# Routing of a mixture-of-experts layer: logits with the gate as the stationary operand, 32x32 transposes on VectorE, and a new order of work

## What is computed

```python
scores = jax.nn.softmax(xf @ gate_w.T, axis=-1)
topk_w, topk_i = jax.lax.top_k(scores, 2)
topk_w = topk_w / (topk_w.sum(-1, keepdims=True) + 1e-20)
combine = jnp.zeros((T, 8)).at[jnp.arange(T)[:, None], topk_i].add(topk_w)
h1 = jax.nn.relu(jnp.einsum('th,ehf->tef', xf, w1) + b1)
eo = jnp.einsum('tef,efh->teh', h1, w2) + b2
y = jnp.einsum('te,teh->th', combine, eo)
shared = jax.nn.relu(xf @ sw1 + sb1) @ sw2 + sb2
return y + shared
```

## Time and profile before

| | before |
|---|---|
| median of 3 runs | 638.89 us (638.68 to 639.09) |
| profiled execution, device time | 639.33 us |
| profiled execution, span | 637.5 us |
| PE busy | 606.4 us, 95% of the span |
| DVE, ACT, POOL busy | 441.2, 402.4, 368.5 us |
| mean granted TensorE clock | 0.981 |

### The profile page before, as it was taken

The page is one execution under the profiler, slowest core; times in us unless marked ns, Lnnn a source line. Parts: engine busy times, 40 slices in busy tenths (PEclk is TensorE's granted clock), DMA queues, the critical chain, the costliest instruction groups (busy, mean ns, idle before and its releaser), DMA issues.

```text
span 637.5 us, 17017 instructions
## 1 busy us (share of the span) xinstructions
PE 606.4 (95%) x6275; PEld 529.2 (83%) x6275; DVE 441.2 (69%) x1322; ACT 402.4 (63%) x1346; POOL 368.5 (58%) x545
## 2 busy tenths in 40 slices
PE   8886889999999999999999999999999999999796
PEld 7775779898889888898889889888888889887674
DVE  5453666768777776868777776867777786867553
ACT  3466557676866667676866667675866667666400
POOL 2566437565674847565674847566683856546300
PEclk9988969999999999999999999999999999999999
DMA  6000030120303030120303021030313020020303
GB/s 231 1 27 4 22 97 25 38 97 2 110 26 108 26 105 29 32 103 1 110 26 108 25 100 35 25 111 1 109 27 108 26 81 28 15 97 2 109 2 119
DMA packets 15460, 37.43 MB, mean 59 GB/s; under 512 B 1809, under 2 KB 4241, under 8 KB 15377
## 3 DMA queue, kind: packets, MB, share of 16 engines
q1 hardware_dynamic: 15376, 36.34, 17.1%
HBM read 33.13 MB, written 3.20 MB: 57 GB/s over the span
## 4 chain that ended last, share of the span: by engine, by line
PE 75%; ACT 7%; DVE 7%; POOL 5%; issue 3%; DMA 1%; SPq 0%; ACTq 0%; POOLq 0%; DVEq 0%
PE ps_fill L414 13%; PE ps_fill L416 11%; PE ps_fill L415 11%; PE ps_mix L642 9%; PE ps_dots L630 9%; PE ps_av L650 7%; PE ps_fill L778 6%; PE ps_fill L570 4%; ACT ex L803 3%; DVE aT L1086 3%; POOL sum L1227 2%; PE ps_fill L770 2%; ACT sq L811 2%; POOL sum L1230 1%; PE ps_fill L761 1%
## 5 line engine op out<-in xcount | busy, mean ns | idle before, releaser
L803 ACT ACTIVATE ex<-ps_dots,negmax 128x92 f32<-128x92 f32 x384 | 123.7, 341 | 7.0 <-DVE negmax L1070 6.5
L1227 POOL TENSOR_TENSOR sum<-sq 92x384 f32<-92x384 f32 x64 | 64.2, 1003 | 80.3 <-ACT sq L811 79.5
L1221 POOL TENSOR_TENSOR probs<-ex,rinv 128x552 f32<-128x552 f32 x64 | 71.0, 1109 | 29.7 <-DVE rinv L1076 29.7
L642 PE MATMUL ps_mix<-mixk,probs 64*92 64x64 f32 x1536 | 79.2, 251 | 5.5 <-DVE aT L1086 5.4
L642 PEld LDWEIGHTS ps_mix<-mixk,probs 64*92 64x92 f32 x1536 | 70.7, 163 | 16.3 <-issue 10.7
L1167 DVE SCALAR_TENSOR_TENSOR act<-ps_fill,b_neg,spread 128x368 f32<-128x368 f32 x123 | 67.9, 591 | 19.9 <-PE ps_fill L416 15.1
L803 ACT ACTIVATION_READ_ACCUMULATOR ex<-ps_dots,negmax 128x1 f32 x384 | 81.4, 212 | 0.0
L630 PE MATMUL ps_dots<-xT,yT 128*64 128x92 f32 x1536 | 75.6, 249 | 5.5 <-ACT ex L803 4.9
L630 PEld LDWEIGHTS ps_dots<-xT,yT 128*64 128x64 f32 x1536 | 65.0, 139 | 11.6 <-ACT ex L803 8.8
L1086 DVE TENSOR_TENSOR aT<-ps_mix,arstd 92x384 f32<-92x384 f32 x128 | 64.9, 547 | 7.1 <-ACT arstd L821 5.2
L1244 POOL TENSOR_TENSOR xT<-xT_split_hi,xT_split_lo 128x368 f32<-128x368 f32 x16 | 15.6, 973 | 86.1 <-DVE xT_split_lo L1146 86.1
(11 more groups left out here) (190 smaller groups left out, 1566.9 us busy)
## 6 DMA issues: line engine op xcount, KB each, us to landing
spread<-weights SPq DMA_DIRECT2D x64, 368.0 KB, 5.6
xin<-in_x SPq DMA_DIRECT2D x16, 372.0 KB, 3.2
out<-fT SPq DMA_DIRECT2D x16, 184.0 KB, 1.9
act<-w_raw SPq DMA_DIRECT2D x1, 576.0 KB, 6.5
w_sb<-w_raw SPq DMA_DIRECT2D x1, 576.0 KB, 7.2
qkv<-qk_raw SPq DMA_DIRECT2D x1, 512.0 KB, 5.2
spread<-tok_raw SPq DMA_DIRECT2D x1, 256.0 KB, 3.4
spread<-wv_raw SPq DMA_DIRECT2D x1, 256.0 KB, 5.4
```

The lines of the kernel that those rows point to most:

```text
L642: last = pe.matmul(ps_mix[0:N, half, DH * c:DH * c + DH], probs[rows, (s - 1) % 2, c, :], mixk[rows, :, :].rearrange("p g i -> p (g i)"), ...
L803: last = act.activation(ex[:, s % 2, c, :], ps_dots[:, c // HALF, o:o + N], ACT.Exp, bias=negmax[:, c:c + 1], accum_out=sums[:, s % 2, c:c ...
L1221: pool.tensor_tensor(probs[:, s % 2, :, :], ex[:, s % 2, :, :], rinv[:, s % 2, :].unsqueeze(2).broadcast_to([128, CHUNKS, N]), ALU.mult).t ...
L1227: pool.tensor_tensor(sum4[:, :, :, :], sq[:, :, 0:4, :], sq[:, :, 4:8, :], ALU.add)\
```

## The change

The logits are two products with the gate (padded to 128 columns with zeros) as the stationary operand; x moves, 384 columns each time. They come out with experts in partitions: partitions 0 to 7 hold the gate's high half, 8 to 15 its low half. DVE turns 32x32 blocks (`transpose`), so that 32 partitions hold 12 blocks of rows, adds the two halves, and makes the choice on 12 x 8 = 96 elements per partition. R3 writes three copies of the weights side by side and turns them back with a second `transpose` into `flat`, from which SP stores as before. CT is now a copy on ACT (the high half); a new step CB on DVE makes `combT` out of `flat` and its high half in one instruction. The fill CT and its transposes are gone. `b2_all` has its three copies in partitions 0 to 23 and no longer at 0, 32 and 64; its split takes other instructions. `STEPS`, `BANKS`, `ORDER_0` and `ORDERS_END` are new lists.

```diff
-N_ROUTE = 18
-ROUTED = {"RT": 2, "R2": 12, "R3": N_ROUTE}
+N_ROUTE = 19
+ROUTED = {"RT": 3, "R2": 13, "R3": N_ROUTE}
+SIDE = 32
+BLOCKS = WP // SIDE
-ROWS_CT = (COPIES - 1) * COPY + E
+ROWS_CT = COPIES * E
+STEPS = [('dots', 0), ('mix', 0), ('max', 0), ('sq', 0), ('exa', 0), ('exb', 0), 'Z1', 'Z0', 'Z6', ('av', 0), ('inv', 0),
+ 'Z3', ('ev', 0), ('rstd', 0), 'Z8', 'XE', 'H0', ('scale', 0), 'Z4', 'Z2', ('dots', 1), ('av', 1), ('ev', 1),
+ ('mix', 1), ('sq', 1), ('max', 1), ('exa', 1), 'Z5', 'XO', 'OP', ('exb', 1), ('rstd', 1), 'shift', ('inv', 1), 'V3',
+ ('scale', 1), ('dots', 2), 'TH2', ('max', 2), 'TK', ('mix', 2), 'NH2', 'TH', 'Z7', ('exa', 2), ('exb', 2), 'TX2',
+ 'NH', ('av', 2), 'H1', ('dots', 3), ('sq', 2), 'RT', 'V2', ('inv', 2), 'R2', 'TX', 'R3', 'YF', ('rstd', 2),
+ ('scale', 2), ('ev', 2), 'Y2', 'Y0', 'Y4', 'XS', 'CT', ('max', 3), 'Y6', ('mix', 3), 'Y1', 'CB', ('sq', 3),
+ ('exa', 3), ('exb', 3), 'Y5', 'hold', 'Y3', 'Y7', ('rstd', 3), ('inv', 3), ('scale', 3), ('av', 3), 'BS', 'V0',
+ ('ev', 3)]
-BANKS = [['Z5', 'Z6', 'Z1', 'TK', 'TH', 'V3', 'TX', 'Y5', 'Y1', 'Y0'],
- ['Z3', 'Z8', 'Z7', 'TH2', 'TX2', 'RT', 'CT', 'Y3', 'Y4', 'V0'],
- ['Z2', 'Z0', 'OP', 'Z4', 'V2', 'YF', 'Y6', 'Y2', 'Y7', 'BS']]
+BANKS = [['Z1', 'Z3', 'Z2', 'V3', 'TH', 'TX', 'Y0', 'Y5', 'BS'],
+ ['Z6', 'Z8', 'OP', 'TH2', 'TX2', 'RT', 'YF', 'Y4', 'Y3', 'V0'],
+ ['Z0', 'Z4', 'Z5', 'TK', 'Z7', 'V2', 'Y2', 'Y6', 'Y1', 'Y7']]
...
- ['Z1', 'Z0', 'Z8', 'T2', 'Z3', 'T4', 'T5', 'T6', 'T7', 'YF']]
+ ['Z3', 'Z0', 'Z1', 'T7', 'T4', 'T2', 'T5', 'Z8', 'T6', 'YF']]
...
-        gate_both = sb("gate_both", [128, 2 * E], F32R)
+        gate_both = sb("gate_both", [128, 128], F32R)
...
-                if step == "CT":
-                    pe.wait_ge(route, N_ROUTE * (g + 1))
+                if step == "YF":
+                    pe.wait_ge(combine_ready, g + 1)
...
-                    for t in range(TILES):
-                        x_hi, x_lo = [m[:, R * t:R * t + R] for m in x2T]
-                        o = 2 * E * t
-                        pe.matmul(ps[:, o:o + 2 * E], x_hi, gate_both[:, :], start=True, stop=False)
-                        last = pe.matmul(ps[:, o:o + E], x_lo, gateT[0], start=False, stop=True)
-                    last.then_inc(done, 1)
-                elif step == "CT":
-                    transposes(step, G, [(ps[:, R * t:R * t + R], combine[:, t, :], ident) for t in range(TILES)])
+                    hi, lo = [m[:, :] for m in x2T]
+                    pe.matmul(ps[:, 0:WP], gate_both[:, :], hi, start=True, stop=False)
+                    pe.matmul(ps[:, 0:WP], gate_both[:, :], lo, start=False, stop=True).then_inc(done, 1)
...
+                if step == "CT":
+                    act.wait_ge(weights_flat, g + 1)
+                    at_least(act, combine_ready, g)
+                    act.activation(flat_high[:, :], flat[0:ROWS_CT, 0:W], ACT.Copy).then_inc(combine_high, 1)
-                elif step == "CT":
-                    wait_filled(act, step, G)
-                    act.activation(flat[:, :], ps[0:E, 0:W], ACT.Copy).then_inc(weights_flat, 1)
-                    act.activation(combT[0:ROWS_CT, :], ps[0:ROWS_CT, 0:W], ACT.Copy).then_inc(high_ready[2], 1)
...
-                    sums = bank("RT")[:, 0:2 * TILES * E].rearrange("p (t r e) -> p t e r", t=TILES, r=2)
-                    dve.tensor_reduce(logit[:, :, :], sums, AX_X, ALU.add).then_inc(emptied[BANK["RT"]], 1)
+                    dve.transpose(logits[:, :, :].rearrange("p k e -> p (k e)"), bank("RT")[0:SIDE, 0:WP])\
+                       .then_inc(emptied[BANK["RT"]], 1)
                     wait_emptied(dve, "RT", G)
+                    link(dve.tensor_tensor(logit[:, :, :], logits[:, :, 0:E], logits[:, :, E:2 * E], ALU.add))
...
                     link(dve.tensor_tensor(
-                        rows, key1[:, :, :].unsqueeze(2).broadcast_to([R, TILES, COPIES, E]),
-                        top[:, 7, :].unsqueeze(2).unsqueeze(3).broadcast_to([R, TILES, COPIES, E]), ALU.mult))
+                        chosen[:, :, 0:ROWS_CT].rearrange("p k (r e) -> p k r e", e=E),
+                        key1[:, :, :].unsqueeze(2).broadcast_to([SIDE, BLOCKS, COPIES, E]),
+                        top[:, 7, :].unsqueeze(2).unsqueeze(3).broadcast_to([SIDE, BLOCKS, COPIES, E]), ALU.mult))
+                    at_least(dve, combine_high, g)
+                    at_least(dve, weights_stored, 16 * g)
+                    dve.transpose(flat[:, :], chosen[:, :, :].rearrange("p k e -> p (k e)")).then_inc(weights_flat, 1)
...
+                if step == "CB":
+                    g = G + LAG[step]
+                    dve.wait_ge(combine_high, g + 1)
+                    dve.scalar_tensor_tensor(out=combT[0:ROWS_CT, 0:W], in0=flat_high[:, :].bitcast(F32),
+                                             scalar=lows[:, 2:3], in1=flat[0:ROWS_CT, 0:W], op0=ALU.mult,
+                                             op1=ALU.add).then_inc(combine_ready, 1)
-                elif step == "CT":
-                    dve.wait_ge(high_ready[2], g + 1)
-                    low = combT[COPY:COPY + E, :]
-                    dve.tensor_tensor(low, ps[COPY:COPY + E, 0:W], low.bitcast(F32), ALU.subtract)\
-                       .then_inc(emptied[BANK[step]], 1)
```

More of the change, by code:

```diff
@@ L320, in audio_tower @@
         x2T = split("x2T", [128, WP])
[L321 to L326, removed]
-        key2 = sb("key2", [R, TILES, E])
-        hot2 = sb("hot2", [R, TILES, E])
-        top = sb("top", [R, 8, TILES])
-        combine = sb("combine", [R, TILES, 128])
-        combT = sb("combT", [128, W], F32R)
-        flat = sb("flat", [E, W])
+        logit = sb("logit", [SIDE, BLOCKS, E])
+        shift_l = sb("shift_l", [SIDE, BLOCKS, E])
+        exl = sb("exl", [SIDE, BLOCKS, E])
+        key1 = sb("key1", [SIDE, BLOCKS, E])
+        hot1 = sb("hot1", [SIDE, BLOCKS, E])
+        rest = sb("rest", [SIDE, BLOCKS, E])
+        key2 = sb("key2", [SIDE, BLOCKS, E])
+        hot2 = sb("hot2", [SIDE, BLOCKS, E])
+        top = sb("top", [SIDE, 8, BLOCKS])
+        logits = sb("logits", [SIDE, BLOCKS, SIDE])
+        b2_low = sb("b2_low", [ROWS_CT, 128])
+        chosen = sb("chosen", [SIDE, BLOCKS, SIDE])
+        combT = sb("combT", [128, WP], F32R)
+        flat = sb("flat", [SIDE, WP])
+        flat_high = sb("flat_high", [ROWS_CT, W], F32R)
         spread = sb("spread", [128, E, W])
@@ L390, in audio_tower @@
         xsum_ready = sem("xsum_ready")
-        high_ready = [sem(f"high_ready{k}") for k in range(3)]
+        high_ready = [sem(f"high_ready{k}") for k in range(2)]
         patch_high = sem("patch_high")
@@ L975, in prepare @@
                     wait_filled(dve, "pD")
-                    low = slice((COPIES - 1) * COPY, (COPIES - 1) * COPY + E)
-                    for r in range(COPIES):
-                        rows = slice(COPY * r, COPY * r + E)
-                        last = dve.tensor_tensor(b2_sb[rows, :], bank("pD")[rows, 0:128], b2_sb[rows, :], ALU.add)
-                    last.then_inc(emptied[BANK["pD"]], 1)
-                    wait_emptied(dve, "pD")
-                    for r in range(COPIES):
-                        rows = slice(COPY * r, COPY * r + E)
-                        last = dve.tensor_copy(b2_all[rows, :], b2_sb[rows, :])
-                    last.then_inc(halved, 1)
-                    steps[0] += 1
+                    dve.tensor_tensor(b2_sb, bank("pD")[0:ROWS_CT, 0:128], b2_sb, ALU.add).then_inc(emptied[BANK["pD"]], 1)
+                    wait_emptied(dve, "pD")
+                    dve.tensor_copy(b2_all[0:ROWS_CT, :], b2_sb).then_inc(halved, 1)
+                    dve.wait_ge(halved, steps[0] + 1)
+                    dve.tensor_tensor(b2_low[:, :], b2_sb, b2_all[0:ROWS_CT, :].bitcast(F32), ALU.subtract)\
+                       .then_inc(halved, 1)
+                    dve.wait_ge(halved, steps[0] + 2)
+                    dve.tensor_scalar(b2_low[:, :], b2_low[:, :], lows[:, 0:1], None, ALU.mult).then_inc(halved, 1)
+                    steps[0] += 3
                     dve.wait_ge(halved, steps[0])
-                    dve.tensor_tensor(b2_all[low, :], b2_sb[low, :], b2_all[low, :].bitcast(F32), ALU.subtract)\
+                    dve.scalar_tensor_tensor(out=b2_all[0:ROWS_CT, :], in0=b2_all[0:ROWS_CT, :].bitcast(F32),
+                                             scalar=lows[:, 1:2], in1=b2_low[:, :], op0=ALU.mult, op1=ALU.add)\
                        .then_inc(experts_ready, 1)
@@ L1017, in routing @@
                 g = G + LAG[step]
[L1018 removed]
+                steps = [{"RT": 0, "R2": ROUTED["RT"], "R3": ROUTED["R2"]}[step]]
                 def link(ins):
@@ L1190, in _ @@
             pool.memset(eps[:, :], LN_EPS).then_inc(pool_consts, 1)
-            pool.memset(combine[:, :, :], 0.0)
+            pool.memset(gate_both[:, :].bitcast(F32), 0.0)
+            pool.memset(chosen[:, :, :], 0.0)
             pool.memset(combT[:, :].bitcast(F32), 0.0)
@@ L1300, in layouts @@
```

(6 more changed lines are left out.)

60 lines of the change are left out of this document (28 added, 32 removed), and 9 rows, old and new, of tables (ORDERS_END, STEPS).

## The result

| | before | after |
|---|---|---|
| median | 638.78 us (638.30 to 639.09, 4 runs) | 712.35 us (710.00 to 713.26, 4 runs) |
| span of the profiled execution | 637.5 us | 710.5 us |
| PE busy | 606.4 us, 95% | 640.8 us, 90% |
| DVE busy | 441.2 us | 508.0 us |
| mean granted TensorE clock | 0.981 | 0.923 |

The changed kernel takes 1.1147 times as long (95% interval 1.1119 to 1.1175). A group lasts 40.98 us on average, measured over twelve groups from one RT to the next, against 36.0; 13 x 4.98 = 64.7 of the 73.6 us are lost in the steady groups, and the other 8.8 at the ends.

A forecast was written before the change was run, and what follows sets the result against it. PE was taken as the bound. Period 35.4 + 4.8 (wait) + 3.2 (clock) = 43.4 against 36.0 us, +96 over 13 iterations, plus 8.6 at the ends on 639.3: 744 us, range 640 to 768.

The forecast's parts named there:

- main case: Steady groups: PE waits at Y4 for `fT` and the clock falls behind it; 720 to 768 us, chance 0.45.
- rival 2: POOL holds DVE, but the clock does not fall or PE's idle is shorter; 700, up to 720 us, chance 0.15.
- Rivals 3 and 4: 3: routing done before PE needs the bank, 630 to 636, chance 0.17; 4: gains and ends cancel, 638 to 640, 0.05.
- PE alone: PE's own need per steady group, without waits or clock loss: 35.4 us, between 35.2 and 35.6.
- Lengths on DVE: Routing instructions on DVE: 0.26 us for 96 elements, 0.46 for 288, 0.557 for a transpose.
- Who waits for whom: DVE instructions with two SBUF operands wait for POOL; `fT` is late and Y4 waits for it, 4.8 us per group.
- Rival 1: POOL's lock on DVE matters little: `fT` ends at n+9.0, Y4 idles 0.9 us, clock stays; 652 us, chance 0.18.
- The size of the wait: DVE waits for POOL's running instruction and those queued straight behind it, so `fT` ends at n+12.9 instead of n+9.0.
- n: The moment POOL finishes the `rstd` for which normalization `NH` waits on DVE; the forecast's DVE, POOL and PE times count from it.
- When Y4 is due: PE reaches Y4 at n+8.1 and waits for `fT` to empty YF's bank until n+12.9: 4.8 us idle.
- The clock: Behind PE's idle in each group, half clock over 6.7 us costs 3.2 us, bounds nothing and 5.1.
- The ends: Last iteration: Z1 waits for Z3's activation, YF starts 5.2 us later, half clock 3.4 more: +8.6 us; start taken as nothing.

The follow-up runs named there:

- the run without POOL's reads: The changed kernel, with POOL's H1, sq2, inv2 and first XS instruction only writing constants, leaving those parts of the computation out: 644.13 us.
- The run with PE kept busy: The changed kernel, with PE making the product of Y0 five times over where Y4 waits for `fT`: 680.89 us.
- the kernel with routing aside: The new operations in the order before the change, then steps PE waits for moved ahead of parts of routing and other fills given to banks: 674.52 us.
- the run with copies: The kernel before, with six 128x368 copies on POOL beside each group's routing that nothing reads: 650.17 us in one run.
- the old order: The new operations in the orders and banks of the kernel before, CT no fill, CB behind mix 3: 684.36 us.

## Why the prediction was right, and where its sizes were off

The forecast was 744 us, the result 712.35: slower, by the mechanism that was forecast, inside the range of 640 to 768. But it lies below the 720 to 768 that the forecast gave its own main case, and within the 700 to 720 of rival 2. Half of that rival came true: PE's idle was shorter. The other half, a clock that does not fall, did not. Rivals 3 and 4 are out by the time.

- **PE alone, 35.4 us.** Nearly right. PE is busy 38.25 of the 40.98 us, so it idles 2.73; half of 5.40 us at half clock is 2.70. What is left is 35.55, and PE is busy 35.68 in the run without POOL's reads.
- **Lengths on DVE.** Right. 0.26 was forecast for 96 elements and 0.246 measured where nothing holds them, 0.46 and 0.455 for 288, 0.557 and 0.561 to 0.567 for a transpose. On the transposes the Trainium skill, "Vector Engine (DVE) Microarchitecture Reference", section 3.8, gives a rate of one element per cycle and lane; no run here takes the rate apart, and what the traces show is that a transpose is as dear as a copy of the same 384 columns (0.557).
- **Who waits for whom.** Right: the addition aside, the instructions that begin beside POOL's run are the long ones, Y4 waits for `fT`, and the line without POOL's reads shows the cause. Rival 1, that the lock matters little, is out for the kernel as it was changed.
- **The size of the wait: this step failed.** It stands in "and for those queued straight behind it", taken from the one row at 584.42. In the steady groups DVE waits for one instruction, the one that it begins beside, and gets in ahead of the next. From n = 316.19 the addition ends at n+1.9 and not at n+2.85, R2 at n+7.0 and not at n+7.7, and R3's product, which was to sit out all of XS, gets in behind xT's addition at n+8.7 and not n+10.5. `fT` ends at n+11.2, not n+12.9.
- **When Y4 is due.** n+8.1 was forecast, PE stood still from n+8.9, in part because Y2 waited 0.5 us for the low part of xT, which the layout took to be done. So 2.25 us of idle came out in place of 4.8, plus the 0.5.
- **The clock.** 3.2 us per group were taken, 2.70 measured: it falls in every group, but stays down for 6.8 us in some and 3.4 in others. It falls after an idle of half the forecast length too. The run with PE kept busy measures the same loss another way: 2.3 per group.
- **The ends.** 8.6 forecast, 8.8 measured. The store of the weights to YF takes 14.6 us instead of 6.6; Z1 waits for Z3's activation, as the layout said, and from the last RT to the end it is 8.9 us more. That the sum agrees as well is luck: up to the second RT the changed kernel is 4.3 us faster (112.2 us against 116.5), where the forecast took nothing, and between the last two RTs it is 4.9 us slower (35.9 against 31.0), where the forecast has no term. In the lines of the last iteration the wait stands at the first, the half clock in the second (0.51 us, 0.33 at full clock); the last is YF at full clock:

```profile
694.92 0.67 PE L421 MATMUL ps_fill<-x2T_hi,w_split_hi 128*128 128x368 f32 x1 [8.10 <-DVE act L1172]
695.39 0.51 PE L422 MATMUL ps_fill<-x2T_lo,w_split_hi 128*128 128x368 f32 x1
...
701.80 5.73 PE L771 MATMUL ps_fill<-act,w_sb 128*128 128x368 f32 x18
```

Period by terms: 35.55 + 2.73 + 2.70 = 40.98 where 35.4 + 4.8 + 3.2 = 43.4 was forecast; 13 times the difference is 31 of the 32 us by which the forecast was too high.

## What to carry to other kernels

Before a chain of small instructions is moved on one engine, lay the queue of the engine that can hold it up beside it (here POOL), and count for each instruction with two SBUF operands the neighbour that will be running; here one instruction took 0.25 us in a hole of that neighbour's queue and 0.52 to 1.22 outside. A short wait of TensorE is charged twice where the clock falls behind it: here 2.7 us of waiting cost 5.4. A single row that shows a longer wait than all others of its kind is a bound and not the value to take.

## What the runs showed that was not expected

- POOL's copies and conversions hold DVE's two-input instructions as its sums do. Beside copies 0.18 became 0.40 (above); beside a conversion, line 1037 of the kernel with routing aside took 0.47 us in one group, against 0.24 with POOL idle, so what was expected of conversions ahead of the run with copies was wrong. Only writes without reads left them alone.
- In one of sixteen groups DVE waits for a whole row of POOL instructions, 3.92 us for nine of them, in the others for one. It is the same group, the one that is routed in iteration 15, in seven kernels, the kernel before among them. That iteration has a list of its own; whether this matters no run tells, and the cause stays open.
- The half-clock time comes in lengths of 3.4 and 6.8 us, one or the other in neighbouring groups with the same wait ahead of them; and behind the same 1.9 us of idle, in the old order, the clock falls in eleven groups and not in two.
